# The second norm of a post-norm layer by blocks, with ScalarE's root and one Newton step

## The reference

```python
def _layernorm(x, axis=-1, eps=1e-05):
    m = jnp.mean(x, axis=axis, keepdims=True)
    v = jnp.var(x, axis=axis, keepdims=True)
    return (x - m) / jnp.sqrt(v + eps)

x = _layernorm(x + _L0_attn_ref(x, ...), axis=-1)
x = _layernorm(x + _L0_ffn_ref(x, ...), axis=-1)
```

## Time and profile before

| | us |
|---|---|
| median of 3 runs | 1215.68 (1215.44 to 1216.79) |
| the profiled execution | 1218.6 |
| its span, first to last instruction | 1216.5 |
| first load of the second norm issued | 1186.35 |
| first statistics start | 1189.80 |
| first tile scaled by ScalarE starts | 1197.51 |
| last tile scaled by ScalarE ends | 1213.35 |

### The profile page before, as it was taken

The page is one execution under the profiler, slowest core; times in us unless marked ns, Lnnn a source line. Parts: engine busy times, 40 slices in busy tenths (PEclk is TensorE's granted clock), DMA queues, the critical chain, the costliest instruction groups (busy, mean ns, idle before and its releaser), DMA issues. The chain is left out here.

```text
span 1216.5 us, 23951 instructions
## 1 busy us (share of the span) xinstructions
PE 1147.1 (94%) x8592; PEld 497.6 (41%) x8592; DVE 662.5 (54%) x1802; ACT 873.4 (72%) x1109; POOL 354.0 (29%) x391
## 2 busy tenths in 40 slices
PE   9999999999999999999999989878999999999980
PEld 4332222222222222222222211266777777777760
DVE  5644333232356526635362401457898888888757
ACT  2889999999999999999999998524334334334314
POOL 5421111111122221330322120022464455455340
PEclk9999999999999999999999998979999999999995
DMA  5843331422421332032302100263525743553216
GB/s 177 182 111 75 101 80 44 99 67 78 99 69 61 96 68 74 31 104 78 70 29 83 37 28 7 73 202 48 121 68 85 136 95 49 121 109 48 27 19 276
DMA packets 119296, 104.16 MB, mean 86 GB/s; under 512 B 59223, under 2 KB 104508, under 8 KB 119184
## 3 DMA queue, kind: packets, MB, share of 16 engines
q1 hardware_dynamic: 101720, 76.90, 24.6%
q0 software_dynamic: 15968, 24.12, 9.2%
q10 hardware_dynamic: 1496, 1.68, 0.4%
HBM read 48.07 MB, written 47.96 MB: 79 GB/s over the span
## 5 line engine op out<-in xcount | busy, mean ns | idle before, releaser
L1497 ACT ACTIVATE prob<-ps_s 128x1024 f32<-128x1024 f32 (+4 forms) x841 | 709.3, 1004 | 42.1 <-PE ps_s L1380 40.3
L1397 PE MATMUL ps_o<-prob,v_aug 128*17 128x512 f32 (+3 forms) x3236 | 421.3, 569 | 3.0 <-DVE acc L1581 2.3
L1380 PE MATMUL ps_s<-qop,kop 51*128 51x512 f16 (+3 forms) x1618 | 273.2, 370 | 14.1 <-issue 3.6
L2461 ACT ACTIVATE hid<-ps_h,b 128x384 f32<-128x384 f32 (+1 forms) x192 | 107.3, 560 | 234.4 <-PE ps_h L2404 227.3
L1380 PEld LDWEIGHTS ps_s<-qop,kop 51*128 51x128 f16 x1618 | 66.0, 93 | 399.1 <-ACT prob L1497 360.2
L2420 PE MATMUL ps_y<-w2s,hs 128*128 128x256 bf16 (+1 forms) x1728 | 191.0, 274 | 3.7 <-DVE hs L2502 3.7
L2404 PE MATMUL ps_h<-xs,w1s 128*128 128x384 bf16 (+1 forms) x1152 | 186.8, 316 | 0.0
L1581 DVE COPY acc<-ps_o 32x512 f32<-32x512 f32 (+2 forms) x108 | 74.3, 688 | 206.0 <-PE ps_o L1397 204.4
L2420 PEld LDWEIGHTS ps_y<-w2s,hs 128*128 128x128 bf16 (+1 forms) x1728 | 160.6, 99 | 29.4 <-issue 6.5
L2374 POOL DMA_INDIRECT result<-y,entry x72 | 114.1, 1584 | 184.5 <-DVE y L2491 151.6
L1533 POOL TENSOR_SCALAR_AFFINE_SELECT prob<-prob 128x256 f32<-128x256 f32 (+1 forms) x179 | 68.3, 393 | 311.2 <-ACT prob L1497 309.5
(11 more groups left out here) (203 smaller groups left out, 702.8 us busy)
## 6 DMA issues: line engine op xcount, KB each, us to landing
w<-in_W SPq DMA_DIRECT2D x16, 1024.0 KB, 8.6
slots_x<-empty POOLq DMA_DIRECT2D x12, 520.0 KB, 4.1
qop<-fparts_q SPq DMA_DIRECT2D x42, 128.0 KB, 4.5
aT<-attnT SPq DMA_DIRECT2D x16, 256.0 KB
x_all<-in_x SPq DMA_DIRECT2D x8, 512.0 KB
result<-x_all SPq DMA_DIRECT2D x8, 512.0 KB, 3.3
x_all<-result SPq DMA_DIRECT2D x8, 512.0 KB, 6.5
out<-x_all SPq DMA_DIRECT2D x8, 512.0 KB, 2.6
```

Source lines behind the costliest of these rows:

```text
L1380: mm = pe.matmul(ps_s[:, u.p % SLOTS_S, e, a.q0:], o.key(e, a.h, a.kt), o.query(e, a.h, a.b, a.q0), start=True, stop=True)
L1397: mm = pe.matmul(ps_o[32 * c:32 * c + VW, a.q0:], o.v[:, a.kt, a.h], prob[:, t % RING, c % 2, c // 2, a.q0:], start=a.first, stop=a.last)
L1497: act.activation(prob[:, t % RING, n, e:z, q0:], ps_s[:, u.p % SLOTS_S, e:z, q0:], ACT.Exp, scale=1.0 / (SCALE * SCALE)).then_inc(exp_done, 1)
L2461: act.activation(hid[:, q % HB, 0:w], ps_h[:, q % HB, 0:w], ACT.Gelu_apprx_tanh, bias=b1[:, e, q % HC:q % HC + 1]).then_inc(gelu, 1)
```

## The change

The groups become single blocks, eight of them. VectorE writes v + EPS; ScalarE takes its root with its Sqrt function; VectorE takes the reciprocal as a guess g and makes one Newton step, rstd = g x (1.5 - 0.5 x v x g x g), then nmr. These are five instructions (`finish`). For the first block they stand alone behind one statistic of the next block; for later blocks one step of the next block's `spread` goes behind each of the first four. Those are the rest of the four statistics, and as a fifth step all four aggregates with the addition of EPS, which so stand ahead of nmr. ScalarE issues the root of the next block behind the first two tiles of a block, and gets one small Sqrt ahead of everything, right after the last gelu, in `warm`. The last two tiles of the last block stay with VectorE.

```diff
@@ -2467,7 +2467,7 @@
                 over_experts(act, one)
-                z.scalar(act)
+                z.scalar(act, r.rstd[0:1, 0:1])
...
-    GROUPS = [(0, 1), (2, 3), (4, 5), (6,), (7,)]
-    WIDEST = 2
+    TILES = NB * KT
+    GROUPS = [(n * KT, (n + 1) * KT) for n in range(NB)]
+    BY_VECTOR = KT // 2
+    FINISH = 5
 
     def __init__(z, io, sb, sem, x1_all, result):
         z.z = x1_all
-        z.stats = sb("statsc", [P, 2, z.WIDEST, KT, 6], F32)
-        z.mv = sb("mvc", [P, NB, KT, 2], F32)
-        z.tmp = sb("tmpc", [P, 5, z.WIDEST, KT], F32)
-        z.rstd = sb("rstdc", [P, NB, KT], F32)
-        z.nmr = sb("nmr", [P, NB, KT], F32)
+        z.stats = sb("statsc", [P, z.TILES, 6], F32)
+        z.mv = sb("mvc", [P, z.TILES, 2], F32)
+        z.v = sb("varc", [P, z.TILES], F32)
+        z.root = sb("rootc", [P, z.TILES], F32)
+        z.guess = sb("guessc", [P, z.TILES], F32)
+        z.half = sb("halfc", [P, z.TILES], F32)
+        z.rstd = sb("rstdc", [P, z.TILES], F32)
+        z.nmr = sb("nmr", [P, z.TILES], F32)
+        z.warm = sb("warmc", [1, 1], F32)
         z.src = result.rearrange("(n p s) d -> n p s d", p=P, s=KT)
         z.dst = io["out"].rearrange("o (n p s) d -> (o n) p s d", p=P, s=KT)
         z.loaded = [sem(f"z_loaded{n}") for n in range(NB)]
-        z.step = sem("c_step")
         z.spread_step = sem("spread_step")
+        z.roots = sem("roots")
         z.scales = sem("scales")
         z.applied = sem("applied")
-        z.applied_last = sem("applied_last")
         z.stored = sem("out_stored")
 
     def sync(z, sp):
         for n in range(NB):
             sp.dma_start(z.z[:, n], z.src[n]).then_inc(z.loaded[n], 16)
         for n in range(NB):
-            sp.wait_ge(z.applied, KT * (n + 1) if n < NB - 1 else KT * n + KT // 2)
+            sp.wait_ge(z.applied, KT * (n + 1) if n < NB - 1 else KT * (n + 1) - z.BY_VECTOR)
             if n == NB - 1:
-                sp.wait_ge(z.applied_last, KT // 2)
+                sp.wait_ge(z.scales, z.FINISH * len(z.GROUPS) + z.BY_VECTOR)
             sp.dma_start(z.dst[n], z.z[:, n]).then_inc(z.stored, 16)
         sp.wait_ge(z.stored, 16 * NB)
 
-    def scalar(z, act):
-        for g, blocks in enumerate(z.GROUPS):
-            act.wait_ge(z.scales, g + 1)
-            for n in blocks:
-                for s in range(KT if g < len(z.GROUPS) - 1 else KT // 2):
-                    act.activation(z.z[:, n, s], z.z[:, n, s], ACT.Identity, scale=z.rstd[:, n, s:s + 1],
-                                   bias=z.nmr[:, n, s:s + 1]).then_inc(z.applied, 1)
+    def scalar(z, act, some):
+        act.activation(z.warm[:], some, ACT.Sqrt)
+
+        def root(g):
+            a, e = z.GROUPS[g]
+            act.wait_ge(z.spread_step, 2 * e + g + 1)
+            act.activation(z.root[:, a:e], z.v[:, a:e], ACT.Sqrt).then_inc(z.roots, 1)
+
+        root(0)
+        for g, (a, e) in enumerate(z.GROUPS):
+            act.wait_ge(z.scales, z.FINISH * (g + 1))
+            for i in range(a, min(e, z.TILES - z.BY_VECTOR)):
+                n, s = divmod(i, KT)
+                act.activation(z.z[:, n, s], z.z[:, n, s], ACT.Identity, scale=z.rstd[:, i:i + 1],
+                               bias=z.nmr[:, i:i + 1]).then_inc(z.applied, 1)
+                if i == a + 1 and g + 1 < len(z.GROUPS):
+                    root(g + 1)
 
     def vector(z, dve):
 
-        c = Chain(dve, z.step, 0, RSQRT_STEPS * len(z.GROUPS))
-        d = Chain(dve, z.spread_step, 0, 2 * KT * NB)
-        for s in z.spread(d, 0):
+        d = Chain(dve, z.spread_step, 0, 2 * z.TILES + len(z.GROUPS))
+        for _ in z.spread(d, 0):
             pass
-        for g, blocks in enumerate(z.GROUPS):
+        for g in range(len(z.GROUPS)):
             later = z.spread(d, g + 1) if g + 1 < len(z.GROUPS) else iter(())
-            n0, w = blocks[0], len(blocks)
-            mean, var = z.mv[:, n0:n0 + w, :, 0], z.mv[:, n0:n0 + w, :, 1]
-            rstd = z.rstd[:, n0:n0 + w]
-            tmp = [z.tmp[:, k, 0:w] for k in range(5)]
-            d.wait()
-            for k, _ in enumerate(rsqrt_pieces(c, var, tmp, rstd)):
-                if k >= 3:
+            next(later, None)
+            for _ in z.finish(dve, g):
+                if g:
                     next(later, None)
-            c.wait()
-            dve.scalar_tensor_tensor(out=z.nmr[:, n0:n0 + w], in0=mean, scalar=-1.0, in1=rstd, op0=ALU.mult,
-                                     op1=ALU.mult).then_inc(z.scales, 1)
-            if g == len(z.GROUPS) - 1:
-                n = blocks[0]
-                for s in range(KT // 2, KT):
-                    dve.tensor_scalar(z.z[:, n, s], z.z[:, n, s], z.mv[:, n, s, 0:1], z.rstd[:, n, s:s + 1],
-                                      ALU.subtract, ALU.mult).then_inc(z.applied_last, 1)
             for _ in later:
                 pass
-        c.end()
+        for i in range(z.TILES - z.BY_VECTOR, z.TILES):
+            n, s = divmod(i, KT)
+            dve.tensor_scalar(z.z[:, n, s], z.z[:, n, s], z.mv[:, i, 0:1], z.rstd[:, i:i + 1],
+                              ALU.subtract, ALU.mult).then_inc(z.scales, 1)
         d.end()
 
+    def finish(z, dve, g):
+
+        a, e = z.GROUPS[g]
+        v, root, guess, half, rstd = (t[:, a:e] for t in (z.v, z.root, z.guess, z.half, z.rstd))
+        dve.wait_ge(z.roots, g + 1)
+        dve.reciprocal(guess, root).then_inc(z.scales, 1)
+        yield
+        dve.wait_ge(z.scales, z.FINISH * g + 1)
+        dve.tensor_tensor(root, guess, guess, ALU.mult).then_inc(z.scales, 1)
+        yield
+        dve.wait_ge(z.scales, z.FINISH * g + 2)
+        dve.scalar_tensor_tensor(out=half, in0=root, scalar=-0.5, in1=v, op0=ALU.mult, op1=ALU.mult).then_inc(z.scales, 1)
+        yield
+        dve.wait_ge(z.scales, z.FINISH * g + 3)
+        dve.scalar_tensor_tensor(out=rstd, in0=half, scalar=1.5, in1=guess, op0=ALU.add, op1=ALU.mult).then_inc(z.scales, 1)
+        yield
+        dve.wait_ge(z.scales, z.FINISH * g + 4)
+        dve.scalar_tensor_tensor(out=z.nmr[:, a:e], in0=z.mv[:, a:e, 0], scalar=-1.0, in1=rstd, op0=ALU.mult,
+                                 op1=ALU.mult).then_inc(z.scales, 1)
+
     def spread(z, d, g):
 
         dve = d.eng
-        for v, n in enumerate(z.GROUPS[g]):
-            dve.wait_ge(z.loaded[n], 16)
-            for s in range(KT):
-                d.did(dve.bn_stats(z.stats[:, g % 2, v, s], z.z[:, n, s]))
-                yield
+        a, e = z.GROUPS[g]
+        for i in range(a, e):
+            n, s = divmod(i, KT)
+            if s == 0:
+                dve.wait_ge(z.loaded[n], 16)
+            d.did(dve.bn_stats(z.stats[:, i], z.z[:, n, s]))
+            yield
         d.wait()
-        for v, n in enumerate(z.GROUPS[g]):
-            for s in range(KT):
-                d.did(dve.bn_aggr(z.mv[:, n, s], z.stats[:, g % 2, v, s]))
-                yield
+        for i in range(a, e):
+            d.did(dve.bn_aggr(z.mv[:, i], z.stats[:, i]))
+        d.wait()
+        d.did(dve.tensor_scalar(z.v[:, a:e], z.mv[:, a:e, 1], EPS, None, ALU.add))
+        yield
```

## The result

The changed kernel took 1221.62 us (median of 5 runs, 1219.04 to 1221.75), the kernel before 1215.44 (5 runs, 1214.31 to 1216.79): ratio 1.0039, 95% interval 1.0027 to 1.0051. It is slower, as forecast.

What follows compares the result with a forecast made beforehand. At the kernel's end, VectorE's first group bounds, then ScalarE's own pace. +3.50 in the norm and -0.1 of tail make +3.4 on the profiled execution; with the median 2.9 below profiled time, 1219.1 us, range 1216.9 to 1221.6.

Steps and rivals of the forecast that it cites:

- The loop through the root: Later blocks of the second norm: two tiles, root, VectorE's steps to nmr and handoffs close a loop, 3.29 us a block.
- The first block: Start of the second norm: fewer statistics, aggregates and small steps before ScalarE's first scaling, which starts 4.38 us earlier.
- The sum: Whole end of the kernel: +3.50 at ScalarE's last end, -0.1 of tail, +3.4 us on the profiled execution.
- tail: From ScalarE's last end to the span's end: 3.15 us before, at best 0.1 comes off.
- A stray wait of VectorE for issue: In the second norm, formerly covered by ScalarE's queue, may now fall on the path: 0 to +0.4 us.
- Carrying the difference over: Whole kernel: the runs' median lies 2.9 us below the profiled time, and this was applied to the forecast, giving 1219.1.
- the long root: ScalarE's Sqrt in each block at the upper end of the earlier rows, 0.398 us: +1.0 in the range.
- the gap: An issue gap in the second norm, counted as 0.4 us toward the range's upper end.
- Rival A: Second norm: VectorE's work decides, 2.26 us a block, fewer small steps gain throughout; faster, 1212.6 us; 6%.
- B: Later blocks: the loop exists but is about 0.25 us shorter, six times; 1217.6 us, +1.9; 13%.
- C: ScalarE's later blocks: Sqrt and Identity each load a table, +11, 1230 us; about 1250 at 2.66 a switch; 4%.
- D: Later blocks: a longer loop, root at 0.398 us, +1.0, and an issue gap; 1220.5 us; 17%.

Runs made afterwards that it cites:

- the change again: The changed kernel run once more with no edit, against the kernel before: 1219.84 us over 12 runs, ratio 1.0030.

## Why the prediction was right, and where it was off

- **The loop through the root**, the step that carried the forecast, is shown by the four kernels that lengthen, shorten or open it with the same work in them. I had 3.29 a block and it is 3.22: the root takes 0.19 behind a tile, not the 0.23 that I took from the earlier trace rows, and the two handoffs take 0.03 each, not 0.04 (1196.26 to 1196.29, 1198.26 to 1198.29). From reciprocal to nmr it is 1.81 (1196.29 to 1198.11, 1.82), as summed from the earlier trace rows.
- **The first block.** 3.33 from the first statistic to ScalarE's start, measured 3.29. The first statistic itself came 3.63 after the first load's issue, 0.18 later than before; over the ten traces it varies from 3.43 to 3.90, whatever the kernel.
- **The sum.** ScalarE's last end was to come 27.05 after the first statistic and came at 26.56: five loops 0.35 shorter, block 1 0.09 earlier. The first load's 0.18 and a tail of 3.20 instead of 3.05 take 0.33 of that back, so the norm is +3.24 and I had +3.4. A stray wait of VectorE for issue, for which I had left 0 to +0.4, doesn't appear after.
- **Carrying the difference over** is the step that was mis-sized. I took 2.9 us between the profiled execution of before and the median as something constant. But the executions of before at its clock, 0.974, average 1218.20, and those at 0.978 1215.04, about where the median lay: most of the 2.9 was a draw. Of the 6.2 us between the two medians of the first comparison, the norm accounts for 3.2; three of the five runs of the changed kernel fell in the group at 0.973, and the highest of the five before is at 1216.79, so by the groups' averages the rest is the same draw the other way. That is argued from the groups, not shown run by run. That the first median still lay on the range's end, and not beyond it, is luck: of the terms that reach to 1221.6 neither the long root (1.0) nor the gap (0.4) occurred, and the draw ahead of the norm took their place. Had I known the spread ahead of the norm (1181.7 to 1186.5), the range would have been wider on both sides.
- **Rival A** was wrong for this kernel and right as a description of what lies behind the loop: 2.26 a block by my count, 2.21 in the kernel with the root ahead, though ScalarE's six tiles at the end keep 0.8 us of its gain. **B** would have had the loop 0.25 shorter; it is 0.07 shorter. **C** did not occur: one table load for Sqrt, at 1170.37, beside ScalarE's idle time, and none at the tiles. From the last gelu's end (1170.35) to the warm root (1171.66) this switch took 1.31 us, so C's dearer price, with 2.66 a switch, would have been too high here. **D**'s root of 0.398 did not occur either; all eight lie at 0.19 to 0.20.
- **Fewer steps on VectorE.** 65 fell to 48 and the norm grew. The Trainium skill, "VectorE: DVE Perf Modes", section "Rules for kernel authors", asks for fewer operations and not fewer semaphores; the runs agree where no wait on another engine closes a loop: from single blocks with the old steps, 104 of them, to the 48 with the root ahead the norm falls from 34.98 to 28.26. Through the loop, from 65 to 48, it grows from 30.15 to 33.39.
- **A pointer as bias.** The root went from 0.20 to 0.28 or 0.30. The Trainium skill, "ScalarE: Activation LUTs", section "What ACT_TABLE_LOAD costs", gives about 93 ns for each such operand; the traces agree, with 0.08 to 0.10.

## What to carry to other kernels

When two engines hand work to each other, write down the circle: from a result of one through the other's queue, in program order, back to what that result needed. If the circle for one block is longer than the busier engine's work for it, moving an instruction in a queue is worth more than removing some: here 1.0 us a block, 5.1 in all. Look at both engines' waits together. Idle time on one says only that something is slow; idle time on both, for one another and in every block, was here the sign of a loop. Compare traces by the stage that was changed, since here the rest varied more than the change.

## What the hardware showed that was not expected

The same instructions ahead of the norm took from 1181.7 to 1186.5 us. One part of it is whether TensorE, after being idle for 3.7 of the 6 us from 829, goes on at 2.4 GHz or spends part of the next 6 us at 1.2 GHz (granted clock 1.00 or 0.72 there), which costs 1.0 to 1.6 us. The other lies in the first 20 us. Here are two executions of the changed kernel, the first one and the one of the change again:

```profile
5.00:20.00 15.00, 15.00 (x99) 6.59 (x78) 7.98 (x17) 3.20 (x5) 8.64 (x15) 0.89 0.52 151
5.00:20.00 15.00, 15.00 (x99) 6.95 (x84) 10.43 (x21) 3.20 (x5) 10.66 (x17) 1.00 0.66 190
```

TensorE is busy throughout in both, after little work in the first 2 us (0.60 busy). In four of the ten traces its clock is 0.89 here, and the table load ahead of the first gelu starts at 803.66 to 804.28; in the six where it is 1.00, at 800.45 to 803.03. Why one execution gets the one and not the other isn't shown.
